# Attention: the maxima's rows turned in 32x32 blocks on VectorE, the output divided as summed and carried as rows

## The reference, cut to what matters

```python
q, k, v = ...                                       # (b, h, s, hd) from src @ q_w, k_w, v_w
scores = einsum('bhqd,bhkd->bhqk', q, k) / sqrt(hd) * scale[..., None]
aw = softmax(scores, axis=-1)                       # exp(s - max) / sum
out = einsum('bhqk,bhkd->bhqd', aw, v).transpose(0, 2, 1, 3).reshape(b, s, d)
gate = sigmoid(out @ gate_w + gate_b)
attn = out * gate @ out_w
x = _ln(src + attn, n1_g, n1_b)                     # then the router and the experts
```

## Time and profile before

| | us |
|---|---|
| three executions | 2483.32, 2482.34, 2487.67 |
| median | 2483.32 |
| span of the profiled execution | 2487.7 |
| TensorE busy | 2369.6 (95%) |
| VectorE busy | 2102.9 (85%) |
| ScalarE busy | 1796.4 (72%) |
| GpSimd busy | 992.7 (40%) |

### The profile page before, as it was taken

One profiled execution on the slowest core, in us unless ns is written; L12 is line 12 of the kernel. 1 busy time (PEld: TensorE's weight loads), 2 busy tenths in 40 slices (PEclk: granted clock), 3 DMA queues, 4 the chain that ended last, 5 costly groups with the idle time before them and its releaser, 6 DMA issues. The chain is left out here.

```text
span 2487.7 us, 45337 instructions
## 1 busy us (share of the span) xinstructions
PE 2369.6 (95%) x16331; PEld 1028.3 (41%) x16331; DVE 2102.9 (85%) x4156; ACT 1796.4 (72%) x2368; POOL 992.7 (40%) x1186
## 2 busy tenths in 40 slices
PE   7899999999689999999999999999999999996996
PEld 5566655655443223223222222223223222473663
DVE  6778788989689999999998999898899996283886
ACT  4888887777334887878787787787787878762664
POOL 1687878888741222211221221221211011255664
PEclk8999999999889999999999999999999999997998
DMA  3322233223240220304012030040040000125892
GB/s 110 112 88 90 85 92 105 89 99 96 67 137 14 37 43 7 59 14 65 14 31 35 14 59 7 14 65 2 14 65 2 2 2 24 52 83 204 297 304 101
DMA packets 105956, 174.09 MB, mean 70 GB/s; under 512 B 21218, under 2 KB 80658, under 8 KB 100596
## 3 DMA queue, kind: packets, MB, share of 16 engines
q1 hardware_dynamic: 98996, 156.08, 23.6%
q0 software_dynamic: 6016, 14.49, 1.7%
q10 hardware_dynamic: 720, 0.62, 0.1%
HBM read 145.21 MB, written 27.02 MB: 69 GB/s over the span
## 5 line engine op out<-in xcount | busy, mean ns | idle before, releaser
L1682 DVE TENSOR_REDUCE max_part<-round_psum 128x1 f32<-128x512 f32 x2048 | 1269.0, 683 | 101.8 <-PE round_psum L1591 96.8
L1647 ACT ACTIVATE p_exp<-score_psum 128x1024 f32<-128x1024 f32 x1024 | 993.3, 1022 | 213.7 <-PE score_psum L1576 209.3
L1591 PE MATMUL round_psum<-k_stack,q_stack 64*128 64x512 bf16 x2048 | 705.5, 384 | 10.7 <-DVE max_part L1682 6.5
L1567 PE MATMUL score_psum<-q_stack,k_stack 64*128 64x512 bf16 x2048 | 599.0, 379 | 0.9 <-ACT p_exp L1647 0.2
L1576 PE MATMUL score_psum<-q_stack,k_stack 35*128 35x512 bf16 x2048 | 594.6, 378 | 0.0
L1622 PE MATMUL pv_psum<-p_exp,values 128*17 128x512 f32 x4096 | 539.6, 598 | 0.0
L1591 PEld LDWEIGHTS round_psum<-k_stack,q_stack 64*128 64x128 bf16 x2048 | 189.4, 93 | 600.3 <-DVE max_part L1682 510.7
L672 PE MATMUL rot<-tokens_t,w_in 128*128 128x512 f32 x576 | 271.7, 603 | 0.2
L1576 PEld LDWEIGHTS score_psum<-q_stack,k_stack 35*128 35x128 bf16 x2048 | 188.9, 94 | 116.0 <-issue 0.5
L1729 POOL TENSOR_TENSOR rden<-pv_out,minus_one 128x16 f32<-128x16 f32 x31 | 90.0, 2903 | 332.4 <-ACT pv_out L1665 330.1
L1715 POOL CAST max_parts<-max_neg 128x16 bf16<-128x16 f32 x96 | 20.4, 212 | 365.8 <-DVE max_neg L1688 343.4
(11 more groups left out here) (300 smaller groups left out, 3472.9 us busy)
## 6 DMA issues: line engine op xcount, KB each, us to landing
cum_rows_in<-cum_rows SPq DMA_DIRECT2D x64, 512.0 KB, 3.8
expert_w<-in_expert_w SPq DMA_DIRECT2D x24, 1028.0 KB
tokens_t<-in_expert_w SPq DMA_DIRECT2D x15, 1028.0 KB
cum_pairs_in<-cum_rows SPq DMA_DIRECT2D x240, 64.0 KB, 2.8
qk_rows<-qk_parts SPq DMA_DIRECT2D x64, 192.0 KB, 3.1
q_stack<-qk_rows SPq DMA_DIRECT2D x84, 128.0 KB, 8.1
k_stack<-qk_rows SPq DMA_DIRECT2D x84, 128.0 KB, 9.1
token_rows<-tokens SPq DMA_DIRECT2D x12, 512.0 KB, 3.7
```

The costliest lines, as they stand in the source:

```text
L1567: nc.tensor.matmul(ebank[i // 2][:, i % 2, :], ks[rows, n % 2, plane, k * P:(k + 1) * P], qs[rows, n % 2, plane, q * BLK:(q + 1) * BLK], s ...
L1591: nc.tensor.matmul(bank[step][:, :], qs[rows, n % 2, plane, at:at + P], ks[rows, n % 2, plane, keys * BLK:(keys + 1) * BLK], start=True, s ...
L1647: nc.scalar.activation(pt[:, (k * 2 + pair) % 4, :, :], ebank[pair][:, :, :], ACT.Exp).then_inc(*exped.up(u, k, pair))
L1682: nc.vector.tensor_reduce(mx[:, c * HG + h, keys:keys + 1], bank[step][:, :], AX_X, ALU.max).then_inc(*maxed.up(u, k, i))
```

## The change

**The rows of the maxima.** The parts get a fourth, zero row (`MWIDE`), and the columns of the maxima are ordered by `max_column` so that after a transpose of each 32x32 block on VectorE (`nc.vector.transpose`, 128x64 bf16) the wanted rows lie in blocks. SP stores them to DRAM in four DMAs, waits for these, and loads `q_stack` in four DMAs of 3 x 16 pieces of 32 elements. `turn_rows` moves from two steps to one step behind `negate`. The transpose on TensorE and the copy on ScalarE are gone.

**The output** is not turned. SP stores the four denominator rows (`out_low`, phase 2), loads them as 128x16 (`out_column`, phase 3), GpSimd inverts them and SP stores the inverses (`out_inverse`, phase 6), SP loads each row spread over its 16 partitions (`out_spread`, phase 8), GpSimd multiplies 128x512 and SP carries the result by four DMAs to the place where the gate's product wants it (`out_rows`, phase 11). For the last unit TensorE spreads the denominators by a product with one column of the identity, and VectorE takes the reciprocal of 128x512 and multiplies.

**The gate stage** reads this place (`oT`) instead of its own turned copy; the `turn` words are gone from the lists of TensorE and ScalarE. The normed rows are written to the same memory by blocks (`xr_block`) and saved in two DMAs per block instead of one.

**Ring.** `turn_rows` and `turn_out` are no users of the three banks any more.

```diff
@@ attention_order
-        plan(u * KT - LEAD + KT + 1, ("turn_rows", u, 0, 0))
-        plan(u * KT + KT + 2, ("turn_out", u, 0, 0))
+        plan(u * KT - LEAD + KT, ("turn_rows", u, 0, 0))
+        for wait, what in OUT_AT:
+            plan(u * KT + KT + wait, (what, u, 0, 0))
...
+OUT_AT = (2, "out_low"), (3, "out_column"), (6, "out_inverse"), (8, "out_spread"), (11, "out_rows")
+def max_column(h, c):
+    return h // 2 * 2 * CPB + c * 2 + h % 2
@@ attention: users of the ring
-    users = [step for step in order if step[0] in ("max", "turn_rows", "turn_out", *splits)]
+    users = [step for step in order if step[0] in ("max", *splits)]
@@ SP
                 if what == "turn_rows":
                     n, q = UNITS[u]
-                    sp_.wait_ge(*rows_stored.at(u))
+                    sp_.wait_ge(*rows_turned.at(u))
+                    for pb in range(P // SQ):
+                        nc.sync.dma_start(rows_dram[u % 2, :, pb, :, :], mturn[pb * SQ:(pb + 1) * SQ, :]
+                                          ).then_inc(*rows_saved.up(u, pb))
+                    sp_.wait_ge(*rows_saved.at(u, P // SQ - 1))
+                    blocks = rows_dram[u % 2].rearrange("c pb (h r) (two i) -> h two r (c pb) i", r=MWIDE, two=2)
                     for h in range(HG):
-                        nc.sync.dma_start(qs[MROWS_AT[h % 2], n % 2, rest_of(h)[1], q * BLK:(q + 1) * BLK],
-                                          mrow[h * MROWS:(h + 1) * MROWS, u % 2, :]).then_inc(*max_row[u % 2].up(u, h))
+                        nc.sync.dma_start(qs[MROWS_AT[h % 2], n % 2, rest_of(h)[1], q * BLK:(q + 1) * BLK]
+                                          .rearrange("r (c i) -> r c i", i=SQ),
+                                          blocks[h % 2, h // 2, 0:MROWS, :, :]).then_inc(*max_row[u % 2].up(u, h))
+                if what == "out_low" and u < NU - 1:
+                    sp_.wait_ge(*pv_out.at(u))
+                    for h in range(HG):
+                        low = h * 32 + HD
+                        nc.sync.dma_start(den_dram[u % 2, h:h + 1, :],
+                                          pvs[low:low + 1, :]).then_inc(*den_saved.up(u, h))
+                if what == "out_column" and u < NU - 1:
+                    sp_.wait_ge(*den_saved.at(u, HG - 1))
...
+                    nc.sync.dma_start(rden[:, :], den_dram[u % 2].rearrange("h (a w) -> (h a) w", w=CPB * HG)
+                                      ).then_inc(*den_load.up(u))
+                if what == "out_inverse" and u < NU - 1:
+                    sp_.wait_ge(*inverse.at(u))
+                    nc.sync.dma_start(inv_dram[u % 2].rearrange("h (a w) -> (h a) w", w=CPB * HG),
+                                      rden[:, :]).then_inc(*inv_saved.up(u))
+                if what == "out_spread" and u < NU - 1:
+                    sp_.wait_ge(*inv_saved.at(u))
...
+                    for h in range(HG):
+                        nc.sync.dma_start(rspread[h * 32:h * 32 + HD, :], inv_dram[u % 2, h:h + 1, :].to_broadcast([HD, BLK])
+                                          ).then_inc(*spread.up(u, h))
+                if what == "out_rows":
...
+                    sp_.wait_ge(*(divided if u < NU - 1 else last_divided).at(u))
+                    for h in range(HG):
+                        row = (g % 2) * HG * HD + h * HD
+                        nc.sync.dma_start(oT[row:row + HD, g // 2, b * SEQ + q * BLK:b * SEQ + (q + 1) * BLK],
+                                          pvs[h * 32:h * 32 + HD, :]).then_inc(*out_saved.up(u, h))
@@ TensorE (turn_rows and turn_out gone)
+                if what == "out_low" and u == NU - 1:
                     pe.wait_ge(*pv_out.at(u))
...
+                        m = nc.tensor.matmul(ebank[0][h * 32:(h + 1) * 32, 0, :], K["ident"][:, low:low + 1].to_broadcast([P, 32]),
+                                             pvs[:, :], start=True, stop=True, skip_group_check=True)
@@ ScalarE (copies of turn_rows and turn_out gone)
                     if u:
-                        act.wait_ge(*divided.at(u - 1))
+                        act.wait_ge(*out_saved.at(u - 1, HG - 1))
@@ VectorE
+                if what == "turn_rows":
+                    if u == 0:
+                        ve.wait_ge(*padded.at(0))
+                    ve.wait_ge(*part_of.at(u, MROWS - 1))
+                    if u:
+                        ve.wait_ge(*rows_saved.at(u - 1, P // SQ - 1))
+                    nc.vector.transpose(mturn[:, :], mparts[:, :, :].rearrange("p n r -> p (n r)")
+                                        ).then_inc(*rows_turned.up(u))
+                if what == "out_inverse" and u == NU - 1:
...
+                    nc.vector.reciprocal(rspread, ebank[0][:, 0, :]).then_inc(*last_inverse.up(u))
                     ve.wait_ge(*last_inverse.at(u))
+                    nc.vector.tensor_tensor(pvs[:, :], pvs[:, :], rspread, ALU.mult).then_inc(*last_divided.up(u))
@@ GpSimd
+                if what == "out_inverse" and u < NU - 1:
...
+                    po.wait_ge(*den_load.at(u))
+                    nc.gpsimd.tensor_tensor(rden[:, :], rden[:, :], minus[:, :].to_broadcast([P, CPB * HG]),
+                                            ALU.pow).then_inc(*inverse.up(u))
+                if what == "out_rows" and u < NU - 1:
+                    po.wait_ge(*spread.at(u, HG - 1))
+                    nc.gpsimd.tensor_tensor(pvs[:, :], pvs[:, :], rspread, ALU.mult).then_inc(*divided.up(u))
@@ gate stage, TensorE
-                        if c == 0:
-                            pe.wait_ge(*heads_t.at(b, k))
-                        m = nc.tensor.matmul(gbank[c][:, :], w_gate[:, k, c * P:(c + 1) * P], oT[:, two, k, :],
+                        if (b, c, k) == (0, 0, 0):
+                            pe.wait_ge(*G.out_saved.at(NU - 2, HG - 1))
+                        if (b, c, k) == (NBLK - 1, 0, 0):
+                            pe.wait_ge(*G.out_saved.at(NU - 1, HG - 1))
+                        m = nc.tensor.matmul(gbank[c][:, :], w_gate[:, k, c * P:(c + 1) * P],
+                                             oT[:, k, b * BLK:(b + 1) * BLK],
```

More of the change, by code:

```diff
@@ L1604, in _ @@
                     m.then_inc(*v_summed.up(c))
[L1605 to L1613, removed]
                 if what == "weigh":
@@ L1626, in _ @@
                             m.then_inc(*weighed.up(u, k, h // 2))
-                if what == "turn_out":
+                if what == "out_low" and u == NU - 1:
                     pe.wait_ge(*pv_out.at(u))
[L1629 to L1632, removed]
+                    pe.wait_ge(*exped.at(u, KT - 1, 1))
+                    for h in range(HG):
+                        low = h * 32 + HD
+                        m = nc.tensor.matmul(ebank[0][h * 32:(h + 1) * 32, 0, :], K["ident"][:, low:low + 1].to_broadcast([P, 32]),
+                                             pvs[:, :], start=True, stop=True, skip_group_check=True)
+                    m.then_inc(*last_spread.up(u))
                 if what in splits:
@@ L1863, in gate_and_route @@
     halves = [(b, i) for b in range(NBLK) for i in range(2)]
-    t_users = [(what, b) for what, b in order["PE"] if what in ("turn", "rows")]
-    t_before = {u: t_users[i - 1] for i, u in enumerate(t_users) if i}
     filled = sems.dma("records_filled", [0])
-    turned = sems.events("heads_turned", halves)
-    heads_t = sems.events("heads_t_stored", halves)
     gate_in = sems.events("gate_summed", halves)
@@ L1919, in on_sync @@
                 sp_.wait_ge(*xr_in.at(b))
-                nc.sync.dma_start(tokens_dram[:, c, 0:D], attn[:, c, :]).then_inc(*xr_saved.up(b))
+                for half in range(2):
+                    g = b * CPB + 2 * half
+                    nc.sync.dma_start(tokens_dram[:, g:g + 2, 0:D], xr_block(b)[:, half, :, :]).then_inc(*xr_saved.up(b, half))
     def on_scalar(act):
         for what, b in order["ACT"]:
-            if what == "turn":
-                for k in range(KD):
-                    act.wait_ge(*turned.at(b, k))
-                    if b >= 2 and k == 0:
-                        act.wait_ge(*gated.at(b - 2, 1))
-                    nc.scalar.copy(oT[:, b % 2, k, :], tbank[k][:, :]).then_inc(*heads_t.up(b, k))
             if what == "source":
@@ L2005, in on_tensor @@
                 for half in range(2):
-                    last, lb = t_before[what, b]
-                    pe.wait_ge(*(heads_t if last == "turn" else xr_t).at(lb, half))
+                    if b:
+                        pe.wait_ge(*xr_t.at(b - 1, half))
                     if half == 0:
```

105 lines of the change are left out of this document (44 added, 61 removed), and 8 rows, old and new, of the table STAGE5.

## The result

The changed kernel takes 2493.69 us (median of nine runs, 2491.63 to 2504.22), the kernel before 2486.91 (nine runs, 2482.34 to 2489.00); the ratio is 1.0034, 95% interval 1.0023 to 1.0046. So the change costs about 8.5 us (0.0034 x 2487), 0.3%: slower, as forecast, but by 8.5 us and not by 30. The two medians alone differ by 6.8 us, which lies inside the interval; I go by the ratio. The profiled execution spans 2491.4 us against 2487.7.

What follows compares the result with a forecast made beforehand. VectorE and TensorE were taken as both nearly full in attention. Terms -17.4 - 6.0 + 9.6 + 11 + 8.8 + 15 + 0.7 + 8.3 = +30.0 on the 2483.3 us median gave 2513, range 2476 to 2550.

Steps and rivals of the forecast that it cites:

- rival B: Attention: rows land in time, denominators get through between stacks, (4) and (5) cost nothing; +6, 2489 us; chance 0.20.
- (1): Attention: VectorE's idle gaps at the turns of output and rows go in 30 units, -17.4 and -6.0 us.
- (2): Attention: VectorE gets a block transpose per unit at 0.32 us, 30 units, +9.6 us.
- rival E: Attention: VectorE's gaps stay because a step's loop takes up what is freed; 2537 us; chance 0.05.
- (3): Units where `low` or `scale` meets the negation: VectorE's transpose waits for GpSimd's parts, +10 and +1 us.
- (7): The end, last sums copy to gate stage: longer division, SP's queue and a slower clock, less turns saved; +8.3 us.
- (4): Rows' round trip through DRAM: takes 7.7 us, lands late, 0.4 us in each of 22 units, +8.8 us.
- rival D: Attention: each small transfer costs more, rows 1.6 us late in 22 units, stacks 5 each; 2549 us; chance 0.15.
- (5): Seven units with stack transfers: the denominator's path queues between them, five units lose 3 us each, +15 us.
- (6): Unit 31, the last: the rows' trip is longer, partly offset by an earlier transpose and a lost ScalarE copy; +0.7 us.
- +4 for the clock: Part of (7): after some 14 us idle, TensorE runs at half speed in the gate stage, +4 us.
- -4 for the turns: Part of (7): six more turns of 0.87 us leave the gate stage's chain, counted as 4 us saved.

Runs made afterwards that it cites:

- the doubled one: The changed kernel with the VectorE transpose of the maxima's parts run twice, the first into a spare tile: ratio 1.0043.
- the rows alone: The kernel before with only the change's part for the rows of the maxima, the output turned and divided as before: 2486.17 us, ratio 1.0006.
- the doubled run: The changed kernel with each unit's rows of the maxima stored to DRAM twice ahead of their loads, one copy unused: 2558.31 us, ratio 1.0292.
- the run with the parts first: The changed kernel with negation and GpSimd's parts first in their step, the output's product and rows two steps later: 2481.3 us, ratio 0.9982.

## Why the prediction was right in its sign and wrong in its size

The time that came is rival B's (rows in time, denominators through between the stacks, 2489), to which I gave 0.20; the measured 8.5 us over 2483.3 are 2492. That B's number is so near is in part luck: its sum gains 10 us too little by the gaps and has the collisions 7 us too cheap. By the steps of the prediction:

- **(1) the gaps, (2) the transpose.** Both gaps closed; rival E is out. The two terms were -13.8 for 30 units; found are -0.76 in each of 31 (mean of the clean ones), -23.6. The transpose costs 0.12 (the doubled one), not 0.32: behind the negation of the earlier trace rows, my nearest row, the next maximum waits for the negation by a semaphore, and behind the transpose none does. That this is why they differ I have not tested. The gaps were then worth 0.88 and not the 0.78 of idle that the rows show, nearly all of the difference at the gap of 0.20 (the rows alone gained 0.17 net, so 0.29). One reason can be read from the rows: maxima of 0.68 us start every 0.62, so each overlaps the one ahead by 0.06, and a gap costs that much more than the idle time in it. This mis-sizing is 10 of the missing 21 us.
- **(3) the collision.** The wait of VectorE came at its place and size, 2.5 us four times, and 1.1 for group 3. What I left out is TensorE's clock. I had priced half speed in (7) but not here: TensorE stops for 2.33 us with VectorE, is then granted 0.50 for 3.4 us, and each collision loses another 1.6. TensorE waits for the rows for 0.3 us at most in the four. Found is 4.1 a unit, 16.4 in four, and 1.35 for group 3: 7 us more than the +11.
- **(4) the rows' trip**, +8.8, is nothing. From the transpose's start (1974.11) to the start of the last load (1979.07) it takes 5.0 us; I had 5.5 up to there and 2.2 for the landing. The load's issue is 0.32 us, not the 0.45 taken from the earlier trace rows; SP is released 1.1 after the last store's issue ended; and in the doubled run TensorE goes on 1.5 us after the start of the last load, so the landing is no longer than that. Forecast 0.5 late, found 1.3 early: the room is real but narrow, as the 64 us of the doubled stores show. The Trainium skill (DMA: Bandwidth & Descriptors, Specifications) has transfers under 512 bytes as read-modify-write. Here stores of 128 bytes a partition had landed 1.75 us after the last one's issue began, and loads of 64-byte pieces 1.5 us after theirs, both at or under the short ends of the earlier trace rows, so no run here shows a price for it, and the argument that I drew from it for rival D did not hold.
- **(5) the stacks**, +15: the denominator's path, 13 to 14.5 us from the copy to the end of the product in clean units (I had 17), takes up to 35 beside the stacks (I had 27 to 31). But its lateness costs little: the product may end 1.3 us after the negation without harm, since VectorE wants the parts at 2.7 and they take 1.4. It cost one wait of 1.05, and once 1.4 us through SP's stores. The larger loss, 4.6 us, was in the one interval of 49.45 us, through SP's order: the split's save stands ahead of the rows, TensorE waits 2.55 for them, and the clock falls (44.90 when the order was changed).
- **(6)** +0.7, found -0.6: nothing.
- **(7) the end**, +8.3: found +10.8 to the boundary and -2.3 behind it. The first part is well forecast: copy to boundary 14.7 where I had 15.1, and 15.5 to the first gate product where I had 16.2. The reciprocal took 3.36 us where I had 4 (and 3.7 by the lower slope); moving the gate loads gave back 4.0. The +4 for the clock was too much: behind the boundary it stays at 0.50 for 5.0 us, and in the kernel before it fell there too, for 3.4, so the change adds 0.8. Of the -4 for the turns, the first sigmoid of the gate shows 1.5 (5.9 us after the boundary before, 4.5 after). The -2.3 is not shown to be an effect of the change: from the boundary to the end two kernels with turns took 344.2 and 342.1, nine without 341.4 to 347.8.

These pieces make the -0.8 of the attention: -23.6 for the gaps, +16.4 and +1.35 for (3), +1.3, +1.4 and +4.6 for (5), and -2.3 in the longer units, which gained a little more than clean ones.

The failed steps are the prices of (2), (4) and (5), 33 us together, against some 11 found. In (2) and (4) I gave a new small operation the price of the nearest row with its surroundings; in (4) and (5) I added waits in line without asking how late each may be. The gaps of (1) were worth 4 us more than I had. Term (3) was 7 us too cheap, for want of the clock, which hid a part of the other errors.

## What to carry to other kernels

A new step on an engine's queue costs by its neighbours more than by itself: list for each queue, DMA issue queues too, what stands ahead of the item that someone waits for. Here the same work, sent in another order, went from 1.0034 to 0.992 of the time before. Ask of every late result how late it may be; a wait forecast on a path with room costs nothing, and a path with 1.3 us of room a unit costs 64 when 2.6 are added. And look at the granted clock behind every stop of TensorE: here a wait of 2.5 us cost 4.1. Another order, which took these waits away, gave back both parts.

## What the runs showed of the hardware

- A block transpose of 128x64 bf16 on VectorE: 0.23 us long, 0.12 us of the queue's time, less than a negation over as many elements (0.32), for which the next instruction waits.
- A reciprocal of 128x512 f32 from PSUM: 3.36 us, 6.6 ns an element, where a maximum over as many takes 0.68.
- Four stores of 32 partitions x 128 bytes to DRAM release SP 1.1 us after the last issue's end; a load of 64-byte pieces takes 0.32 us to issue, where one of the two from DRAM in the earlier trace rows takes 0.45.
- The stops of TensorE named above in the middle of attention (2.00, 2.30, 2.33, 2.41 and 2.55 us) were each followed by 3.4 us at a granted clock of 0.50, which costs 1.7 us; one of 2.78 us was followed by 7 us at 0.58 on average. After stops of 1.66 and 1.90 us in the run with the parts first no fall came.
